# Attention scores and values in six key tiles of 128, with the 16 keys left over in one single-pass product of split exponentials and split values per head

## The reference, cut to what matters

```python
q = jnp.einsum('btd,hrd->bhtr', x, Q)
k = jnp.einsum('bud,hrd->bhur', x, K)
scores = jnp.einsum('bhtr,bhur->bhtu', q, k) / sqrt(d)
attn = jax.nn.softmax(scores, axis=-1)
ctx = jnp.einsum('bhtu,bud->bhtd', attn, x)
out = jnp.einsum('bhtd,hde->bte', ctx, VO)
```

## Time and profile before

| | |
|---|---|
| median of 3 runs | 576.84 us (575.78 to 579.57) |
| profiled execution | 576.89 us |
| its span, first to last instruction | 575.1 us |
| mean granted TensorE clock | 0.992 |
| TensorE busy | 540.7 us (94%) |
| VectorE busy | 372.9 us (65%) |
| ScalarE busy | 323.0 us (56%) |
| GpSimd busy | 81.6 us (14%) |

### The profile page before, as it was taken

How to read it: one execution, slowest core, us unless ns; L and a number is a source line. 1 busy time by engine, 2 the same in 40 slices (tenths; PEclk the granted TensorE clock), 3 DMA queues, 4 the chain that set the end, 5 groups by cost and what they waited for, 6 DMA issues and landing times.

```text
span 575.1 us, 10345 instructions
## 1 busy us (share of the span) xinstructions
PE 540.7 (94%) x3150; PEld 327.1 (57%) x3150; DVE 372.9 (65%) x899; ACT 323.0 (56%) x726; POOL 81.6 (14%) x97
## 2 busy tenths in 40 slices
PE   0898999999989999999999999999999999997994
PEld 0563444443466766766766766766766766553341
DVE  3856663326776876876876876876876877255472
ACT  0467656755665655655655655655655654656331
POOL 0000000003996011010001001001001001120000
PEclk9999999999989999999999999999999999999998
DMA  7600000003623234234234233223223220000016
GB/s 181 241 0 2 0 1 2 0 15 83 147 79 77 69 82 102 63 80 98 66 80 98 66 79 96 69 78 97 68 77 99 69 77 5 1 1 2 0 27 142
DMA packets 21986, 37.65 MB, mean 65 GB/s; under 512 B 5560, under 2 KB 15224, under 8 KB 21704
## 3 DMA queue, kind: packets, MB, share of 16 engines
q1 hardware_dynamic: 21326, 36.42, 24.5%
q10 hardware_dynamic: 634, 0.90, 0.7%
HBM read 6.07 MB, written 2.41 MB: 15 GB/s over the span
## 4 chain that ended last, share of the span: by engine, by line
PE 86%; DVE 5%; ACT 3%; DMA 2%; issue 1%; SPq 1%; DVEq 0%; ACTq 0%
PE P L790 84%; DMA X<-x 2%; PE P L1116 1%; DVE bst L1400 1%; PE P L1315 1%; SPq L411 0%; ACT act L563 0%; DVE xn L1413 0%; DVE gate_s L1527 0%; DMA Ks<-QKH 0%; DVE mx L1624 0%; ACT g L716 0%; PE P L944 0%; DVE xhat L1472 0%; DVE QKL L1612 0%
## 5 line engine op out<-in xcount | busy, mean ns | idle before, releaser
L1624 DVE TENSOR_REDUCE mx<-P 112x1 f32<-112x392 f32 x448 | 216.2, 557 | 82.5 <-PE P L790 82.2
L668 ACT ACTIVATE PT<-P 112x392 f32<-112x392 f32 x448 | 183.8, 501 | 9.8 <-PE P L790 9.1
L790 PE MATMUL P<-Ks,Qs 96*112 96x392 f32 x448 | 160.7, 363 | 0.2 <-DMA Ks<-QKH 0.2
L790 PE MATMUL P<-Qs,Ks 98*112 98x392 f32 x448 | 154.9, 350 | 0.5 <-ACT PT L668 0.5
L790 PE MATMUL P<-PT,XVs 112*64 112x392 f32 x896 | 153.3, 493 | 0.0
L790 PEld LDWEIGHTS P<-PT,XVs 112*64 112x64 f32 x896 | 62.0, 137 | 71.4 <-issue 71.4
L676 ACT ACTIVATE CT<-P 128x392 f32<-128x392 f32 x32 | 15.9, 497 | 129.6 <-PE P L790 129.5
L790 PEld LDWEIGHTS P<-Qs,Ks 98*112 98x112 f32 x448 | 79.1, 177 | 11.4 <-ACT PT L668 3.1
L790 PEld LDWEIGHTS P<-Ks,Qs 96*112 96x112 f32 x448 | 78.8, 178 | 9.6 <-DVE mx L1624 5.8
L768 POOL TENSOR_TENSOR OUT<-OUT,part 120x448 f32<-120x448 f32 x27 | 31.1, 1152 | 256.6 <-DVE part L1651 256.6
L790 PE MATMUL P<-VBs,CT 128*112 128x130 f32 (+1 forms) x320 | 42.2, 261 | 0.0
(11 more groups left out here) (196 smaller groups left out, 463.6 us busy)
## 6 DMA issues: line engine op xcount, KB each, us to landing
Qs<-QKH SPq DMA_DIRECT2D x64, 98.0 KB, 2.2
Ks<-QKH SPq DMA_DIRECT2D x64, 98.0 KB, 2.2
XVs<-XV SPq DMA_DIRECT2D x32, 196.0 KB, 2.5
Qs<-QKL SPq DMA_DIRECT2D x32, 98.0 KB, 2.1
Ks<-QKL SPq DMA_DIRECT2D x32, 98.0 KB, 2.1
X<-x SPq DMA_DIRECT2D x4, 588.0 KB
wa<-table_a SPq DMA_DIRECT2D x1, 2207.5 KB, 8.2
VBs<-VB SPq DMA_DIRECT2D x32, 65.0 KB, 2.2
```

Source lines behind the costliest of these rows:

```text
L668: nc.scalar.activation(PT[:, u, c * HALF:(c + 1) * HALF], P[0:T, score_bank(2 * u + c), 0:HALF], ACT.Exp, scale=float(D) ** -0.5).then_inc ...
L790: return nc.tensor.matmul(dst, lhsT, rhs, start=start, stop=stop, **more)
L1624: nc.vector.tensor_reduce(mx[:, s % 2, c, t:t + 1], bank(n)[0:T, :], AX.X, ALU.max)\
```

## The change

The keys are cut in six tiles of 128 (KT) and 16 keys left over (LEFT). The score tile of the left-over keys comes first in a head: its weights are the 16 keys eight times over, a 128-column block behind the stack in `Ks`, which GpSimd writes (`last_keys`), for the first two heads behind its splits, and then two heads ahead. ScalarE exponentiates the lower 64 rows for the first half of the queries and the upper 64 for the second, into `E`. GpSimd splits `E` in an F32R part and the rest, in `Z`: 32 rows of each for either half (`split_left`). The values of the left-over keys are split in the same way and laid out so that one F32R product of 128 rows by 128 columns gives all four part products for both halves (`left_operands`; `VL`, copied for each head to `VLs` by SyncE's `fill_left`; `masks` are made by VectorE after `means_set`). That product (`context_left`) comes behind six value tiles and closes the sum in bank 5. TensorE waits for `keys_left` before the first score of a head, and for `left_in` and `z_ready` before the new product; GpSimd's `split_left` waits for two exponentials and for the head before to be done. `turn_values` turns 6 tiles of 128 tokens, and one product with the 16 keys repeated, for which SyncE copies `XL` with each image. `av_done` still counts seven a head.

```diff
--- before.py
+++ after.py
@@ -39,6 +39,10 @@
 OJ, OC = 2, HCOL // 2
+KT = 128
+NK = TOK // KT
+LEFT = TOK - NK * KT
+COPIES = KT // LEFT
 GROUPS = 7
@@ -117,7 +121,8 @@
         VB = sb(ctx, "VB", [128, HEADS, 2 * D + 2])
-        XV = sb(ctx, "XV", [T, B, NT, D])
+        XV = sb(ctx, "XV", [KT, B, NK, D])
+        masks = sb(ctx, "masks", [KT, 4])
         mx = sb(ctx, "mx", [T, 2, 2, NT])
@@ -169,17 +174,25 @@
         reg2 = ExitStack()
-        XVs = sb(reg2, "XVs", [T, 4, NT * D])
+        XVs = sb(reg2, "XVs", [KT, 4, NK * D])
         VBs = sb(reg2, "VBs", [128, 4, 2 * D + 2])
-        PT = sb(reg2, "PT", [T, NT, TOK])
+        PT = sb(reg2, "PT", [KT, NK, TOK])
+        E = sb(reg2, "E", [KT, HALF])
+        Z = sb(reg2, "Z", [KT, HALF], F32R)
+        VLs = sb(reg2, "VLs", [KT, 4, 2 * D], F32R)
         CT = sb(reg2, "CT", [128, HALF])
...
         part = sb(reg2, "part", [OROWS, 3, NT * D])
-        OUT = sb(reg2, "OUT", [OROWS, B, NT * D])
-
-        sb(reg2, "past_norm", [128, 160])
+        whole = sb(reg2, "OUT", [128, B, NT * D])
+        OUT = whole[0:OROWS, :, :]
+
         Qs = sb(reg2, "Qs", [HROWS, 4, TOK], F32R)
-        Ks = sb(reg2, "Ks", [HROWS, 4, TOK], F32R)
+        Ks = sb(reg2, "Ks", [HROWS, 4, TOK + KT], F32R)
+        left = whole[:, 1, 0:B * D].rearrange("p (b d) -> p b d", d=D)
+        left_lo = whole[:, 2, 0:B * D].rearrange("p (b d) -> p b d", d=D)
+        XL = [whole[0:D, 3, b * KT:(b + 1) * KT] if b < B - 1 else whole[0:D, 1, B * D:B * D + KT] for b in range(B)]
+        left_hi = sb(reg2, "left_hi", [KT, B, D], F32R)
+        VL = sb(reg2, "VL", [KT, B, 2 * D], F32R)
         reg2.close()
@@ -252,6 +265,9 @@
         value_in = [sem(f"value_in{s}") for s in range(4)]
+        left_in = [sem(f"left_in{s}") for s in range(4)]
+        masks_set, left_step, left_ready = sem("masks_set"), sem("left_step"), sem("left_ready")
+        z_hi, z_ready, keys_left = sem("z_hi"), sem("z_ready"), sem("keys_left")
         mrow_in = [sem(f"mrow_in{s}") for s in range(4)]
@@ -420,6 +436,8 @@
                                    xhat[h * D:(h + 1) * D, b, :]).then_inc(xf_in[b], 16)
+                sync.dma_start(XL[b].rearrange("p (c k) -> p c k", k=LEFT),
+                               xhat[D:2 * D, b, HALF - LEFT:HALF].unsqueeze(1).broadcast_to([D, COPIES, LEFT])).then_inc(xf_in[b], 16)
@@ -431,14 +449,18 @@
                     sync.wait_ge(qk_lo, keys)
-                for dst, src in ((Ks[0:R, s, :], QKH[rows, 1, i, :]), (Ks[R:2 * R, s, :], QKL[rows, 1, i, :]),
-                                 (Ks[2 * R:3 * R, s, :], QKH[rows, 1, i, :])):
+                for dst, src in ((Ks[0:R, s, 0:TOK], QKH[rows, 1, i, :]), (Ks[R:2 * R, s, 0:TOK], QKL[rows, 1, i, :]),
+                                 (Ks[2 * R:3 * R, s, 0:TOK], QKH[rows, 1, i, :])):
                     sync.dma_start(dst.bitcast(F32), src.bitcast(F32)).then_inc(slot_in[s], 16)
...
                 sync.dma_start(VBs[:, s, :], VB[:, group * 4 + s, :]).then_inc(value_in[s], 16)
+
+            def fill_left(b, s):
+
+                sync.dma_start(VLs[:, s, :].bitcast(F32), VL[:, b, :].bitcast(F32)).then_inc(left_in[s], 16)
@@ -461,6 +483,9 @@
             rows_to_stack(0, 1)
+            sync.wait_ge(left_ready, 2)
+            for s in range(4):
+                fill_left(0, s)
@@ -470,6 +495,7 @@
                     fill_values(b, group, s)
+                    fill_left(b, s)
@@ -635,8 +661,9 @@
                 nc.scalar.activation(XV[:, b, :, 0:D - 1],
-                                     P[0:T, XV_BANK, 0:NT * D].rearrange("p (t d) -> p t d", d=D)[:, :, 0:D - 1],
-                                     ACT.Copy).then_inc(xv_done, 1)
+                                     P[0:KT, XV_BANK, 0:NK * D].rearrange("p (t d) -> p t d", d=D)[:, :, 0:D - 1],
+                                     ACT.Copy)
+                nc.scalar.activation(left[:, b, 0:D - 1], P[0:KT, XV_BANK, NK * D:NK * D + D - 1], ACT.Copy).then_inc(xv_done, 1)
@@ -665,8 +692,15 @@
                 scalar.wait_ge(st_full, HEAD_HALVES * n + 2 * u + c + 1)
-                nc.scalar.activation(PT[:, u, c * HALF:(c + 1) * HALF],
-                                     P[0:T, score_bank(2 * u + c), 0:HALF],
+                if u == 0:
+                    own = slice(c * D, (c + 1) * D)
+                    dst = E[own, :]
+                    if c == 0 and not (isinstance(n, int) and n == 0):
+                        scalar.wait_ge(z_ready, 2 * n)
+                else:
+                    own = slice(0, KT)
+                    dst = PT[:, u - 1, c * HALF:(c + 1) * HALF]
+                nc.scalar.activation(dst, P[own, score_bank(2 * u + c), 0:HALF],
                                      ACT.Exp, scale=float(D) ** -0.5).then_inc(exp_done, 1)
@@ -767,12 +801,58 @@
+            def left_operands():
+
+                pool.wait_ge(xv_done, B)
+                pool.wait_ge(masks_set, 1)
+                nc.gpsimd.memset(left[:, :, D - 1:D], 1.0).then_inc(left_step, 1)
+                pool.wait_ge(left_step, 1)
+                nc.gpsimd.tensor_copy(left_hi[:, :, :], left[:, :, :]).then_inc(left_step, 1)
+                pool.wait_ge(left_step, 2)
+                nc.gpsimd.tensor_tensor(left_lo[:, :, :], left[:, :, :], left_hi[:, :, :].bitcast(F32), ALU.subtract).then_inc(left_step, 1)
+                pool.wait_ge(left_step, 3)
+                nc.gpsimd.tensor_scalar(left[:, :, :], left_hi[:, :, :].bitcast(F32), masks[:, 0:1], None, ALU.mult).then_inc(left_step, 1)
+                nc.gpsimd.tensor_scalar(left_lo[:, :, :], left_lo[:, :, :], masks[:, 1:2], None, ALU.mult).then_inc(left_step, 1)
+                pool.wait_ge(left_step, 5)
+                nc.gpsimd.tensor_tensor(left[:, :, :], left[:, :, :], left_lo[:, :, :], ALU.add).then_inc(left_step, 1)
+                pool.wait_ge(left_step, 6)
+                for h in range(2):
+                    nc.gpsimd.tensor_scalar(VL[:, :, h * D:(h + 1) * D], left[:, :, :], masks[:, 2 + h:3 + h], None, ALU.mult)\
+                      .then_inc(left_ready, 1)
+
+            def split_left(n):
+
+                pool.wait_ge(exp_done, HEAD_HALVES * n + 2)
+                if n:
+                    pool.wait_ge(av_done, 7 * n)
+                nc.gpsimd.tensor_copy(Z[:, :], E[:, :]).then_inc(z_hi, 1)
+                pool.wait_ge(z_hi, n + 1)
+                for own in (slice(32, 64), slice(96, 128)):
+                    nc.gpsimd.tensor_tensor(Z[own, :], E[own, :], Z[own, :].bitcast(F32), ALU.subtract).then_inc(z_ready, 1)
+                pool.wait_ge(z_ready, 2 * n + 2)
+
+            def last_keys(n):
+
+                i, s = n // 4, n % 4
+                pool.wait_ge(slot_in[s], 96 * (i + 1))
+                nc.gpsimd.tensor_copy(Ks[:, s, TOK:TOK + KT].rearrange("p (c k) -> p c k", k=LEFT),
+                                      Ks[:, s, NK * KT:TOK].bitcast(F32).unsqueeze(1).broadcast_to([HROWS, COPIES, LEFT])).then_inc(keys_left, 1)
+
+            for n in range(2):
+                last_keys(n)
+            left_operands()
+            split_left(0)
             for n in range(NH - 3):
+                last_keys(n + 2)
+                split_left(n + 1)
                 add_head(n // HEADS, n % HEADS)
-
+            last_keys(NH - 1)
+
+            split_left(NH - 2)
             pool.wait_ge(join_full, 1)
...
             add_head(B - 1, HEADS - 3)
+            split_left(NH - 1)
@@ -1085,20 +1165,21 @@
-                pe.wait_ge(xf_in[b], 32)
+                pe.wait_ge(xf_in[b], 48)
                 if b == 0:
...
                     mm(P[0:OROWS, OUT_BANK, 0:NT * (D + 1)], Bt("mean", T)[:, 0:OROWS],
-                       XV[:, 2:4, :, :].rearrange("p b t d -> p (b t d)")[:, 0:NT * (D + 1)])
+                       XV[0:T, 2:4, :, :].rearrange("p b t d -> p (b t d)")[:, 0:NT * (D + 1)])
                 else:
...
                     pe.wait_ge(turn_done, 1)
-                for t in range(NT):
-                    last = nc.tensor.transpose(P[0:T, XV_BANK, t * D:(t + 1) * D], XF[:, b, t * T:(t + 1) * T],
-                                               Bt("ident", D)[:, 0:D])
-                last.then_inc(xv_full, 1)
+                for t in range(NK):
+                    nc.tensor.transpose(P[0:KT, XV_BANK, t * D:(t + 1) * D], XF[:, b, t * KT:(t + 1) * KT],
+                                        Bt("ident", D)[:, 0:D])
+                mm(P[0:KT, XV_BANK, NK * D:(NK + 1) * D],
+                   XL[b], Bt("ident", D)[:, 0:D]).then_inc(xv_full, 1)
@@ -1125,8 +1206,10 @@
                     pe.wait_ge(exp_done, k - last_score(j) + 1)
-                mm(P[0:T, score_bank(j), 0:HALF], Ks[:, s, u * T:(u + 1) * T],
-                   Qs[:, s, c * HALF:(c + 1) * HALF]).then_inc(st_full, 1)
+                if u == 0 and c == 0:
+                    pe.wait_ge(keys_left, 4 * i + s + 1)
+                keys = Ks[:, s, (u - 1) * KT:u * KT] if u else Ks[:, s, TOK:TOK + KT]
```

(22 more changed lines are left out.)

## The result

The changed kernel takes 598.03 us (median of 4 runs, 597.39 to 600.84) against 578.21 us before (4 runs, 575.78 to 580.63): ratio 1.033, 95% interval 1.028 to 1.038. The prediction was 587.6 us with a range of 581 to 592. The direction was right, and the loss is nearly twice the one forecast.

The account below looks back on a forecast made before the run. TensorE was taken to bound the attention loop. From 576.9 us, 19.5 for the wait at the first score and 0.8 for the clock were added and 9.6 (32 heads at 0.30) taken off: 587.6 us, range 581 to 592.

Parts of the forecast that it names:

- The stall: Before head 0: the first score waits for GpSimd's first key copy behind its 28 splits, until 182.2; 19.5 us lost.
- Rival A: Start of the attention: the wait for the key copy is absent or hidden, kernel faster at 567.3 us; 4 in 100.
- The clock after it: Head 0: after 19 us idle TensorE starts at the low clock; 0.8 us added (0 to 1.7).
- The new product: End of each head: one F32R product delays the context copy by 0.38 us and costs 0.36 us a head.
- rival E: End of each head: the new product is two instructions, 0.66 us, so nothing is saved, 597 us; 2 in 100.
- Rival B: Heads: the wait is there, but TensorE regains nearly the whole tile, 0.48 us a head, 581.0 us; 12 in 100.
- The step that failed: Scores of each head: 14 products and exponentials as before, TensorE following ScalarE at 0.39 us a pair; 0.30 us saved.
- The period outside 10.4 to 10.6 us: Attention loop: heads were to come 10.5 us apart instead of 10.8; a period outside this band would show the forecast wrong.
- Wider score weights: Score products: loads of 128 columns for 112 priced at 0, since the product's streaming sets the 0.18 us.
- rival C: Score products: the wider weight loads set the pace, 4.9 us more, 592.5 us; 7 in 100.
- Rival D: Score products: 128-column loads are fast, so streaming alone sets the pace, 6.7 us less, 580.9 us; 2 in 100.
- GpSimd's steps: Each head: 2.8 us added on GpSimd beside the 1.1 it uses, covered by TensorE's 10.8 us head.

Follow-up runs that it names:

- early_keys: Changed kernel with GpSimd's key copies, left-over operands and first splits of `E` placed between its 28 splits; 578.53 us, ratio 1.0003 to the kernel before.
- early_third: Changed kernel with GpSimd's key copies, operands and first splits between its 28 splits, and the left-over tile third; 572.57 us, ratio 0.9877 to the kernel before.
- exp_whole: Changed kernel with both left-over exponentials over all 128 rows, each into its own buffer, and one more GpSimd cast a head; 592.26 us in one run.
- product_first: Changed kernel with the single-pass product opening each head's sum, ahead of the six value tiles, instead of closing it; 604.53 us in one run.
- no_product: Changed kernel without the single-pass product, so sums lack the last 16 keys; waits, exponentials, splits and copies stay; 585.9 us in one run.
- before_fill: Kernel before plus four unread products in TensorE's pauses between the attention and second mixture of experts; 577.97 us, ratio 1.0004.

## Why the prediction was right in direction and wrong in size

**The stall: right.** +19.12 us for +19.5. GpSimd's queue is what TensorE waits for, the first score came within 0.4 us of its forecast, and moving the copy took the loss away (`early_keys`). Rival A, no stall, is refuted.

**The clock after it: the number came out, the reason didn't.** It was +0.97 us for +0.8, and the prediction put it down to 19 us of idle time. Early_keys has no such idle time and loses more, 7.76 us for the scores of head 0 against 6.61 before, and early_third, without the stall too, takes no more than the kernel before (6.63). So this stretch varies by over 1 us from trace to trace whether the stall is there or not. That the term fitted is luck.

**The new product: right.** It starts 0.07 us before the last value record ends, as in the earlier trace rows, lasts one record (rival E refuted), and the context copy and the first score came at L + 0.41 and L + 0.49 for +0.43 and +0.43 to +0.50. Its price in the chain, 0.36 us, is what exp_whole shows once the exponentials are evenly spaced. Rival E's time, 597, was met in number only. Rival B, 0.48 us saved, isn't met even by the best order, which saves 0.33 (its sum of 581.0 also leaves out the 0.8 for the clock).

**The step that failed** is "The scores stay 14 products and 14 exponentials a head, with 392 columns each, so neither engine has fewer of them", and with it "From there it follows ScalarE at 0.39 us a pair for two more pairs". The count was right and the pace was not. The 0.39 us were read from TensorE's loads at 283.39 and 284.17, which follow exponentials that all start on partition 0; two of the new ones start on 0 and on 64. They come 0.51 us apart, and the wait falls on the very place where I had written that TensorE just touches ScalarE. The period outside 10.4 to 10.6 us, which I had named as the sign, is what the chain shows. The slower pair costs 0.25 us of the 0.30 saved in a normal head. The first head of each four is a further 0.13 us longer, where the kernel before had 0.05: in both kernels ScalarE's copy of the max rows comes 0.51 us behind the context copy there instead of 0.39, and now TensorE waits for what follows it. On average over 28 heads it leaves 0.03 us (302.80 - 301.99, by 28). Over all heads 1.25 us were saved for 9.6: 8.35 of the 9.8 us by which the sum was off. The lowest saving named, 0.15 us a head, covered a wider score load but no slower exponential. The diff shows the `own` slices, and the rows hold no pair of exponentials with different start partitions: an unseen operation was priced as a seen one, without a bound.

**The rest** is +1.66 us behind the heads, most of it (1.40) at the low clock in the second mixture of experts, on which the prediction had no term. Whether it is the change's doing stays open: from 39 us behind the end of the 28 heads to the end, the mean granted clock was 0.95 before and 0.93 after, and in the experiments it lay anywhere between 0.88 and 0.96, without a rule in the edits that I could find.

**What was priced at nothing.** Wider score weights: products still 0.18 us apart with loads of 192 ns, so rival C is refuted. Rival D too: the F32R loads of 128 columns took 192 ns, more than the 179 of 112 columns. The Trainium skill (TensorE: Matmul & The Clock Gate, section on Fast Weight Load and DoubleRow) has loads of exactly 128 weights fast for a type other than FP32, and doesn't say on which side F32R stands; these loads aren't fast. GpSimd's steps: casts of 0.52 us, two subtractions in 2.12, a key copy in 0.29, 3.85 us of work a head with what it did before (89.18 us busy in 250, by 10.785; forecast 2.8 + 1.1) and no wait for `Z` in the loop. The operands were ready at 187.9 and the first split at 190.6, 1.8 us later than the middle of the forecast; the product of head 0 started at 193.52 (forecast 192.8) without a wait. VectorE's maxima: 556 ns, unchanged.

**Two readings of rows in the prediction were off**, without an effect on the sum. The product behind the first one in the earlier trace rows starts 0.29 us after it (550.08, 550.37); the step of 0.17 is the next one, to 550.54. And the VectorE step of 0.42 us in the earlier trace rows reads one SBUF operand, not two.

## What to carry to other kernels

Where an engine just keeps up with TensorE at one place of a loop, price each instruction there by its start-to-start time, and treat one whose partitions, type or shape the trace doesn't hold as unknown, with a bound; its duration alone (490 ns here, as ever) hides the loss. A helper engine's new step stands behind its whole queue: look at what stands ahead of its first use, not only at its share of the loop. And before giving up a tiling that brings nothing, try the odd tile at another place: moved from first to third, with GpSimd's order mended, this one is 1.2% faster than the kernel before instead of 3.3% slower.

## What the runs showed of the hardware that was unexpected

Two ScalarE instructions of 64 x 392 that start on different partitions (0, then 64) come 0.51 us apart, and so does the next one that starts on 0 again; from the same starting partition it is 0.385 us, whether they have 64 or 128 rows. The overlap of 0.11 us between one's end and the next one's start is what goes.

A weight load that is released late isn't hidden any more: with exponentials 0.51 us apart the pairs of products follow at 0.52 us, though TensorE's own pace is 0.36.

A full-array F32R product ahead of a column-split F32 group costs 0.47 us (product_first). Behind the group it makes a head about 0.3 us longer (no_product against after).

The clock granted behind a pause of 1.65 us differed between two traces whose code up to there is the same: the scores of head 0 took 6.61 us in the kernel before, with a granted clock of 0.65 and 0.50 on the way, and 5.62 in before_fill, where the clock stayed full.

The time of one and the same kernel goes with the mean clock it was granted. The 17 runs of the kernel before beside early_third read 575.9 to 577.9 us at 0.992 or 0.993, 578.7 to 579.9 at 0.987 to 0.989, 582.3 to 583.7 at 0.979 to 0.981 (two more lie between). That is over 1% without any change in the program, so a few runs can't settle half a per cent.
